# An attention and expert layer on one core: a reordered opening, and maxima placed one by one in the first softmax

## What is computed

```python
mod = (silu(c) @ wmod).reshape(4, 6, 1, 128)
sa, ca, ga, sb, cb, gb = (mod[:, k] for k in range(6))
ga = (2 * (ga >= 0) - 1) * max(abs(ga), 0.25)      # gb the same
h = layernorm(x) * (1 + ca) + sa
Q, K, V = h @ Wq.T + bq, h @ Wk.T + bk, h @ Wv.T + bv       # 16 heads of 8
Q, K = rope(Q), rope(K)      # the odd member of each pair becomes 0
att = softmax(where(causal, Q @ K.T / sqrt(8), -1e10))
x = x + ga * ((att @ V) @ Wo.T + bo)
h = layernorm(x) * (1 + cb) + sb
x = x + gb * experts(h)      # 8 slices a token, the top 2 of 16 experts each
```

## Time and profile before

| | |
|---|---|
| median of 3 runs | 442.27 us (441.61 to 442.72) |
| the profiled execution | 441.48 us, of which its span is 439.7 us |
| TensorE busy (matmul) | 353.3 us, 80% |
| VectorE, ScalarE, GpSimd busy | 298.0, 242.2 and 111.2 us |
| mean granted clock of TensorE | 0.953 |

### The profile page before, as it was taken

How to read it: one execution, slowest core, us unless ns; L and a number is a source line. 1 busy time by engine, 2 the same in 40 slices (tenths; PEclk the granted TensorE clock), 3 DMA queues, 4 the chain that set the end, 5 groups by cost and what they waited for, 6 DMA issues and landing times.

```text
span 439.7 us, 7235 instructions
## 1 busy us (share of the span) xinstructions
PE 353.3 (80%) x2652; PEld 164.3 (37%) x2684; DVE 298.0 (68%) x596; ACT 242.2 (55%) x291; POOL 111.2 (25%) x151
## 2 busy tenths in 40 slices
PE   0555386888867978999879969998879798879995
PEld 0532142445534444443444434433545323123122
DVE  7479994575878797777576877786549456943342
ACT  1102023344224786887534868875457887858970
POOL 8334720000524020443250204433130023122000
PEclk9996666999989999999998999999999999989999
DMA  8102410000220182554001715551105155704550
GB/s 291 25 1 68 79 46 24 3 5 0 50 29 2 39 106 71 137 143 110 2 25 31 95 51 141 135 133 22 28 0 73 36 144 160 117 2 121 151 135 24
DMA packets 26847, 31.43 MB, mean 71 GB/s; under 512 B 6454, under 2 KB 17718, under 8 KB 26678
## 3 DMA queue, kind: packets, MB, share of 16 engines
q1 hardware_dynamic: 23740, 28.84, 28.3%
q0 software_dynamic: 3072, 2.13, 2.8%
HBM read 3.47 MB, written 1.05 MB: 10 GB/s over the span
## 4 chain that ended last, share of the span: by engine, by line
PE 53%; DVE 19%; ACT 10%; issue 7%; SPq 4%; DMA 4%; POOL 1%; ACTq 0%; DVEq 0%; POOLq 0%
PE acc L1125 17%; PE big L1125 17%; PE misc L1125 17%; ACT ring L657 7%; DVE mx L897 6%; DVE xn L838 3%; DMA q_dense<-nm 2%; PE misc L1144 2%; SPq L425 2%; SPq L446 1%; ACT qk_turned L665 1%; SPq L380 1%; DVE stats L813 1%; DMA q_dense<-qk 1%; ACT L690 1%
## 5 line engine op out<-in xcount | busy, mean ns | idle before, releaser
L657 ACT ACTIVATE ring<-big 128x1024 f32<-128x1024 f32 (+1 forms) x224 | 197.3, 932 | 124.5 <-PE big L1125 123.2
L897 DVE TENSOR_REDUCE mx<-misc 128x1 f32<-128x320 f32 (+7 forms) x154 | 86.9, 589 | 36.0 <-PE misc L1125 34.6
L1125 PE MATMUL acc<-ring,cb 128*32 128x512 f32 x512 | 68.8, 612 | 5.4 <-ACT ring L657 4.4
L1125 PE MATMUL big<-tstack,w1s 128*128 128x512 bf16 x177 | 52.4, 381 | 10.0 <-ACT ring L657 7.1
L1125 PE MATMUL big<-q_dense,k_block 128*128 128x448 bf16 (+7 forms) x249 | 53.4, 320 | 5.2 <-DMA q_dense<-nm 3.1
L1125 PE MATMUL misc<-k_dense,q_block 128*128 128x384 bf16 (+7 forms) x171 | 43.6, 318 | 6.4 <-DVE mx L897 5.9
L1020 DVE SCALAR_TENSOR_TENSOR gm<-acc,cb,gm 128x512 f32<-128x512 f32 x40 | 29.9, 747 | 27.3 <-DMA gm<-wT 14.5
L1125 PEld LDWEIGHTS big<-q_dense,k_block 128*128 128x128 bf16 x256 | 30.8, 148 | 31.1 <-ACT ring L657 14.3
L1125 PEld LDWEIGHTS misc<-k_dense,q_block 128*128 128x128 bf16 x174 | 21.3, 149 | 52.1 <-DVE mx L897 37.0
L1125 PE MATMUL acc<-ring,vals 128*32 128x64 f32 (+7 forms) x512 | 40.1, 421 | 0.4
L1125 PE MATMUL big<-earlier_query,identb 128*128 128x64 bf16 (+2 forms) x176 | 37.0, 210 | 2.5 <-DMA q_dense<-nm 1.8
(11 more groups left out here) (160 smaller groups left out, 486.2 us busy)
## 6 DMA issues: line engine op xcount, KB each, us to landing
gm<-wT SPq DMA_DIRECT2D x64, 256.0 KB
tstack<-tp SPq DMA_DIRECT2D x18, 128.0 KB, 5.1
k_block<-qk_turned POOLq DMA_DIRECT2D x48, 32.0 KB, 3.6
q_dense<-qk SPq DMA_DIRECT2D x24, 64.0 KB
ca<-in_pack_a SPq DMA_DIRECT2D x1, 1155.0 KB, 5.4
k_dense<-qk SPq DMA_DIRECT2D x18, 64.0 KB
xs<-in_x SPq DMA_DIRECT2D x4, 256.0 KB, 8.0
q_block<-qk_turned SPq DMA_DIRECT2D x24, 32.0 KB
```

Source lines behind the costliest of these rows:

```text
L657: act.activation(dst, src, func, scale=scale).then_inc(s["ring_read"], 1)
L897: dve.tensor_reduce(mx[:, g, k:k + n, blk], src, AX.X, ALU.max).then_inc(s["misc_read"], 1)
L1125: return pe.matmul(dst, lhsT, rhs, start=start, stop=stop)
```

## The change

Packs and tables: the condition and `wmod` get a pack of their own (`pack_c`, 772 columns). Maxima go one to a slot, a slot being behind one unit of scores or one weighing, with two behind the first two weighings of a group. `ALONE` has 39 units instead of 33; 7 instead of 13 of row 0 and 31 instead of 30 of row 1 are woven; 15 instead of 16 are left.

```diff
-A_COLS, A_W = columns(("we", P), ("wd", P), ("wv", D), ("cos", T), ("sin", T), ("be", 1), ("bd", 1),
-                      ("cT", NB), ("wmod", 6 * D), ("bv", D))
+A_COLS, A_W = columns(("we", P), ("wd", P), ("wv", D), ("cos", T), ("sin", T), ("be", 1), ("bd", 1), ("bv", D))
+C_COLS, C_W = columns(("cT", NB), ("wmod", 6 * D))
...
-ALONE = UNITS0[0] + UNITS0[1][:3] + [("mT", 0)] + UNITS0[1][3:10]
-REST = UNITS0[1][10:] + [("mT", 1)]
...
+ALONE = UNITS0[0] + UNITS0[1][:3] + [("mT", 0)] + UNITS0[1][3:16]
+REST = UNITS0[1][16:] + [("mT", 1)]
...
+SLOTS = [("scores", 0, 4), ("scores", 0, 5), ("weigh", 0, 0), ("weigh", 0, 1), ("scores", 0, 6), ("scores", 0, 7),
+         ("scores", 0, 8), ("weigh", 0, 2), ("weigh", 0, 3), ("scores", 0, 9), ("scores", 0, 10), ("weigh", 0, 4),
+         ("weigh", 0, 5), ("scores", 0, 11), ("scores", 1, 0), ("scores", 1, 1), ("weigh", 0, 6), ("weigh", 0, 7),
+         ("scores", 1, 2), ("scores", 1, 3), ("scores", 1, 4), ("scores", 1, 5), ("weigh", 1, 0), ("weigh", 1, 1),
+         ("scores", 1, 6), ("scores", 1, 7), ("scores", 1, 8), ("weigh", 1, 2), ("weigh", 1, 3), ("scores", 1, 9),
+         ("scores", 1, 10), ("weigh", 1, 4), ("weigh", 1, 5), ("scores", 1, 11)]
+TWICE = [("weigh", 0, 0), ("weigh", 0, 1), ("weigh", 1, 0), ("weigh", 1, 1)]
+FIRST_SLOTS = SLOTS[:5]
+WOVEN, at = {}, 0
+for slot in FIRST_SLOTS:
+    n = 2 if slot in TWICE else 1
+    WOVEN["first", slot] = REST[at:at + n]
+    at += n
+assert at == len(REST)
+at = 0
+for slot in SLOTS[5:]:
+    n = 2 if slot in TWICE else 1
+    WOVEN["second", slot] = MAXIMA[at:at + n]
+    at += n
+LEFT = MAXIMA[at:]
...
+FOLD_AT, CUT_AT = len(WOVEN) // 2 - 1, [len(WOVEN) // 2 + 2 + k for k in range(4)]
...
+FROM_SCALAR = 4
```

```diff
-            sp.dma_start(ca[:, :], pack_a).then_inc(s["a_loaded"], 16)
             xv = x.rearrange("b (t p) d -> p b t d", p=P)
             sp.dma_start(xs[:, 0], xv[:, 0]).then_inc(s["x0_loaded"], 16)
+            sp.dma_start(cc[:, :], pack_c).then_inc(s["c_loaded"], 16)
+            sp.dma_start(ca[:, :], pack_a).then_inc(s["a_loaded"], 16)
+            sp.dma_start(xs[:, 1], xv[:, 1]).then_inc(s["x1_loaded"], 16)
             sp.dma_start(w1f, w1_rows).then_inc(s["w1_loaded"], 16)
             sp.dma_start(cb[:, :], pack_b).then_inc(s["b_loaded"], 16)
-            for b in range(1, NB):
+            for b in range(2, NB):
...
-                for c, a in Q_BLOCKS[1]:
+                for c, a in Q_BLOCKS[1][0 if b else FROM_SCALAR:]:
                     block_diagonal(sp, q_block_of[b], c, a, PARTS_L[c], 0, "q_block1")
...
-            sp.wait_ge(s["cleared"], 2)
+            sp.wait_ge(s["cleared"], 1)
             stack_k(0)
-            sp.wait_ge(s["zeroed"], 2)
+            sp.wait_ge(s["zeroed"], 1)
             stack_q_block(0)
+            sp.wait_ge(s["cleared"], 3)
             stack_q(0)
-            sp.wait_ge(s["zeroed"], 4)
+            sp.wait_ge(s["spare_cleared"], 2)
             stack_k(1)
             stack_shift(0, [0])
             stack_q_block(1)
```

```diff
+            pool.memset(nought[:, :], 0.0).then_inc(s["nought_ready"], 1)
+            pool.memset(q_block[:].rearrange("r p a t -> r (p a t)").bitcast(F32), 0.0).then_inc(s["zeroed"], 1)
             for t in (later_key, earlier_query, ident, identb):
                 pool.memset(t[:, :], 0.0)
...
             pool.wait_ge(s["shapes_ready"], 7)
-            pool.memset(k_block[:].rearrange("r p a t -> r (p a t)").bitcast(F32), 0.0).then_inc(s["zeroed"], 1)
-            pool.memset(q_block[:].rearrange("r p a t -> r (p a t)").bitcast(F32), 0.0).then_inc(s["zeroed"], 1)
-            pool.wait_ge(s["zeroed"], 2)
+            pool.wait_ge(s["zeroed"], 1)
...
             pool.sem_inc(s["gm_ready1"], CREDIT["gm_ready1"])
             rsqrt(0, 0)
-            pool.memset(tstack[:].rearrange("r p t -> r (p t)").bitcast(F32), 0.0).then_inc(s["zeroed"], 1)
-            pool.memset(gm[:, GMS // 2:GMS, :].rearrange("p k t -> p (k t)"), 0.0).then_inc(s["zeroed"], 1)
             rsqrt(1, 0)
-            pool.wait_ge(s["zeroed"], 4)
             stack_q(0)
             pool.wait_ge(s["ones_loaded"], 16)
             stack_k(0)
             k_blocks(K_BLOCKS)
+            pool.wait_ge(s["spare_cleared"], 2)
+            stack_q(1)
             pool.wait_ge(s["b_loaded"], 16)
-            pool.wait_ge(s["x_loaded"], 16 * (NB - 1))
             pool.wait_ge(s["x0_loaded"], 16)
+            pool.wait_ge(s["x1_loaded"], 16)
+            pool.wait_ge(s["x_loaded"], 16 * (NB - 2))
             pool.wait_ge(s["gates_filled"], 2)
             fold_out(0)
-            stack_q(1)
             stack_k(1)
```

```diff
-            act.wait_ge(s["a_loaded"], 16)
-            act.activation(sil[:, 0, :], A["cT"], ACT.Exp, scale=-1.0).then_inc(s["exp_ready"], 1)
-            act.wait_ge(s["gates_filled"], 1)
-            for k in range(2):
-                act.activation(gabs[k], big[:, 1 + k, :].rearrange("p (b d) -> p b d", b=NB), ACT.Abs)\
-                   .then_inc(s["abs_ready"], 1)
+
+            def clear(t, ready):
+
+                act.copy(t, nought[:, 0:1].to_broadcast([P, t.shape[1]])).then_inc(s[ready], 1)
+
+            act.wait_ge(s["nought_ready"], 1)
+            clear(k_dense[:].rearrange("r p t -> r (p t)").bitcast(F32), "cleared")
+            clear(vals[:].rearrange("q p s w -> q (p s w)"), "cleared")
+            act.wait_ge(s["c_loaded"], 16)
+            act.activation(sil[:, 0, :], C["cT"], ACT.Exp, scale=-1.0).then_inc(s["exp_ready"], 1)
+            clear(q_dense[:].rearrange("r p t -> r (p t)").bitcast(F32), "cleared")
+            clear(k_block[:].rearrange("r p a t -> r (p a t)").bitcast(F32), "k_block_cleared")
+
+            def take_gates():
+
+                act.wait_ge(s["gates_filled"], 1)
+                for k in range(2):
+                    raw = big[:, 1 + k, :].rearrange("p (b d) -> p b d", b=NB)
+                    act.activation(gabs[k], raw, ACT.Abs).then_inc(s["abs_ready"], 1)
+                    act.copy(graw[k], raw).then_inc(s["abs_ready"], 1)
+
+            def stack_q_block():
+
+                act.wait_ge(s["zeroed"], 1)
+                act.wait_ge(s["qk_turned"], 3)
+                for c, a in Q_BLOCKS[1][:FROM_SCALAR]:
+                    block_diagonal(act, q_block, c, a, PARTS_L[c], 0, "q_block1")
 
             def transform(kind, phase, u, src, dst, func, scale):
                 act.wait_ge(s["ring_filled"], phase[0] + u + 1)
@@ -723,6 +767,10 @@
             act.wait_ge(s["shapes_ready"], 1)
             load_table(ACT.Exp)
             turn(0)
+            stack_q_block()
+            clear(tstack[:].rearrange("r p t -> r (p t)").bitcast(F32), "spare_cleared")
+            clear(gm[:, GMS // 2:GMS, :].rearrange("p k t -> p (k t)"), "spare_cleared")
+            take_gates()
             turn(1)
```

```diff
-            here = ("first", 0)
+            here, ahead = ("first", 0), ("second", 0)
             dve.wait_ge(s["x0_loaded"], 16)
             norm_link = links("ln_link", LN_LINKS, 0)
             statistics(xs[:, 0], 0, 0, 0, norm_link)
+            silu()
             normalise(xs[:, 0], 0, 0, norm_link)
+            modulation()
+            pick_modulation(0, 0)
+            dve.wait_ge(s["a_loaded"], 16)
             modulate(0, hT, here, "xT", 0)
             wait_read(dve, here, "xT")
-            dve.wait_ge(s["x_loaded"], 16 * (NB - 1))
+            dve.wait_ge(s["x1_loaded"], 16)
             norm_link = links("ln_link", LN_LINKS, 1)
             statistics(xs[:, 1], 1, 1, 0, norm_link)
             rotate(here, 0)
             cut_rotated(0)
             normalise(xs[:, 1], 1, 0, norm_link)
+            ones_for_sums()
             values(here, 0)
-            ahead = ("second", 0)
             modulate(0, hT, ahead, "xT", 1)
-            fold_gates()
             rotate(ahead, 1)
-            cut_weights()
             maxima(here, 0, ALONE[:4])
             cut_rotated(1)
             maxima(here, 0, ALONE[4:])
-            for at, uses in WOVEN.items():
+            for k, (at, uses) in enumerate(WOVEN.items()):
                 if at[0] == "first":
                     maxima(here, 0, uses)
                 else:
                     maxima(ahead, 1, uses)
+                if k in (FOLD_AT, FOLD_AT + 1):
+                    fold_gates(k - FOLD_AT)
+                if k == FOLD_AT + 1:
+                    dve.sem_inc(s["gates_filled"], 1)
+                if k in CUT_AT:
+                    cut_weights(CUT_AT.index(k))
+            dve.wait_ge(s["x_loaded"], 16 * (NB - 2))
```

```diff
+            pe.wait_ge(s["shapes_ready"], 2)
+
+            def gates():
+                pe.wait_ge(s["sil_ready"], 2)
+                for k, at in enumerate((2, 5)):
+                    for b in range(NB):
+                        ins = matmul(big[:, 1 + k, D * b:D * b + D], silb[:, b, :], C["wmod"][:, D * at:D * at + D])
+                ins.then_inc(s["gates_filled"], 1)
...
 
             here = ("first", 0)
             norm1(here, 0)
```

(22 more changed lines are left out.)

109 lines of the change are left out of this document (56 added, 53 removed).

## The result

| | before | after |
|---|---|---|
| median | 442.22 us (441.61 to 442.72, 4 runs) | 430.13 us (428.60 to 432.79, 4 runs) |
| the profiled execution | 441.48 us, span 439.7 | 431.06 us, span 429.2 |
| mean granted clock | 0.953 | 0.939 |

The ratio is 0.973 (0.969 to 0.977): 12.1 us faster, where 422.0 us was forecast with a range of 417.0 to 427.5. The time is above the range.

The account below looks back on a forecast made before the run. The prediction saw the opening as one chain, then VectorE setting the pace, then TensorE bounding the first softmax. Terms -15.4, -3.6, -1.1 and 0 sum to -20.1 us, giving 422.0 us, range 417.0 to 427.5.

Parts of the forecast that it names:

- Opening, -15.4: From the start to hT of row 0: hT would start at 11.4 instead of 26.79 us, -15.4 us.
- Stacking, -3.6: From hT to the first shifts: faster q_block issue, with folds and cuts moved away, brings the first reduce sooner, -3.6 us.
- not full, so I take issue for the limit: In stacking: DMA engines busy 0.66 at the densest, so issuing transfers was taken to set the pace, behind the -3.6 us.
- the transfers set the stacking: Rival on stacking: transfers, not their issue, are the limit; -1.2 for -3.6 us, total 424.4 us, chance 0.15.
- First softmax, -1.1: First shifts to SP's release: fewer units and waits, less a new stop and slower clock, sum -1.1 us.
- the folds and cuts give back 0.5: In the first softmax: folds and cuts between reduces return 0.5 us of the waits saved, leaving -3.0 us.
- The stop: Ahead of the first softmax: TensorE stands waiting for the second row's stacks, +1.6 us.
- The clock's +1.6: In the first softmax: the stop postpones full clock, some 4.2 us of work at half clock instead of 1, +1.6 us.
- The rival with the stop and the cuts dear (+2.5): Rival on the first softmax: stop and cuts cost more, +2.5 for -1.1 us, total 425.6 us, chance 0.09.
- Behind the release, 0: After SP's release to the end: SP's issues are the same, so no change, 0 us.
- What is gained before 114.6 us stays gained: For everything behind SP's release: no later work is tied to a fixed time, so earlier gains persist unless a new wait eats them.
- signs of being wrong: hT after 15 us, first maxima 10 us after the turned copies, or over 43 us from first scores to SP's release.

Follow-up runs that it names:

- e4: The changed kernel with all eight q_block transfers of row 0 on SP again, none from ScalarE: 428.1 us.
- e6: The changed kernel with row 0's q_dense transfers held back on SP until q_block has landed: 430.4 us.
- e7: The changed kernel with both q_dense and GpSimd's k_block transfers held back until q_block has landed: 431.9 us.
- e2: The kernel before with only the new weave of single maxima and the stop ahead of the softmax, keeping the old opening: 439.8 us.
- e14a: The changed kernel with SP, ScalarE and VectorE held at the start by an extra GpSimd fill of 2048 columns: 431.7 us.
- e14b: The changed kernel with SP, ScalarE and VectorE held at the start by an extra GpSimd fill of 4096 columns: 433.1 us.
- e9: e7 with VectorE's second cut behind 16 instead of 4 of the maxima that run alone: 425.8 us.
- e11: The change with q_dense and k_block held back, later second cut, folds and W1 cuts behind lone maxima, later stack wait, SP issuing ScalarE's q_block transfers: 424.0 us.

## Why the prediction was wrong

- **Opening, -15.4: right** (-15.7), with its parts: fills at 1.9 us, xn at 1.11, tokens at 3.65 us, hT at 11.1.
- **Stacking, -3.6: wrong, and the largest miss.** The step that failed is "not full, so I take issue for the limit". A DMA share of 0.66 is a mean over sixteen engines, and it does not say that a transfer lands no later when others follow it. e4, e6 and e7 show landing as the limit. The issues that were moved up brought the q_dense transfers up behind q_block, and these took back what they gave. The rival "the transfers set the stacking" had the cause, but at -1.2 it took the landing to be no later than before. The first maxima came 10.8 us behind the turned copies (22.67 to 33.43) instead of 9.7 (38.43 to 48.10), which ate most of the 1.2 us that VectorE gained, and from the first reduce to the first shifts it took 17.2 instead of 16.7 us, with 0.9 us of waiting for q_dense ahead of the second cut. I had named that wait and not priced it.
- **First softmax, -1.1: wrong by 2.6 us.** The step that failed is "the folds and cuts give back 0.5", mis-sized by a factor of ten: 5.0 us by the change against e2, with as much time at half clock (6.5 and 6.6 us). The other terms together were too dear: without folds and cuts the sum is -1.6, and e2 measured -3.5. The stop cost 2.0 us where 1.6 was forecast. The clock's +1.6 was too much: e2 has 1.6 us more at half clock than the kernel before, which by the prediction's own half is 0.8. How the rest divides over units and waits stays open. The rival with the stop and the cuts dear (+2.5) named the mechanism, and the stretch came at +1.5. How much of that shows in one profile is in part luck: in e4, e14a and e14b, with the same waits for maxima, the stretch was 1.5 us shorter.
- **Behind the release, 0: wrong by 3.3 us.** "What is gained before 114.6 us stays gained" overlooked that the clock is not part of the work. In 19 profiles with this work unchanged, but for one unit of maxima, the stretch took 324.7 to 328.4 us. Why the clock falls more often in the change stays open.

The misses add up: 3.9 + 2.6 + 3.3 - 0.3 = 9.5 us between -20.1 and the profiled -10.4 us, with rounding. The range failed because two steps missed the same way and the stretch behind had no bounds at all. Two of the prediction's own signs of being wrong came: the first maxima over 10 us after the turned copies, and 44.1 us from first scores to release.

## What to carry to other kernels

Work on a second engine costs what stands still while it runs: the same 7.5 us of VectorE cost 4.4 to 5 us between single reduces and nearly nothing in the gap where that engine waited anyway. Before more queues are given to a set of transfers, ask what the queues will send next: hold back what is not yet due, and then see what waits for the transfers held back, for both sides have to be moved together (e7 lost, e9 won). And a stretch of unchanged work should have a range of its own, here some 4 us on 325, as the clock that it meets may differ.

## What was not expected of the hardware

- The same twelve transfers of 32 KB, last issued at about 26.5 us, were all usable at 29.5, 31.1 or 33.4 us (up to 34.8 in other executions with the same queues), by what was issued behind them, also where that came from another engine's queue. The DMA share was at most 0.73 in the windows of 2 us between 22 and 34 us of the change.
- Taking a queue away made the landing 1.5 us sooner, or more, as SP's next transfers went out 2.8 us later (e4); with those held back, it made the landing 0.8 us later (e11).
- Behind a stop of 2.0 us of TensorE that began 0.8 us after its clock had risen, the clock fell (the change); in e14a, where it rose just as the stop began, it did not, and the softmax was 1.5 us shorter. Further on, the same gap of work lowered the clock at one time and not at another.
